# The experts' second product in five fp32r passes of split weights and channels, with the channels' transpose moved ahead of it in each turn

## What is computed

```python
def body(acc, ew):
    w13_e, w2_e, e = ew
    coef = jnp.sum(jnp.where(topk_ids == e, topk_w, 0.0), axis=-1)
    h = _silu_and_mul(x @ w13_e.T)
    acc = acc + (h @ w2_e.T).astype(jnp.float32) * coef[:, None]
    return (acc, None)
...
x = x + 0.5 * _L0_ffn_ref(_layernorm(x, axis=-1), ...)
x = x + _L0_attn_ref(_layernorm(x, axis=-1), ...)
x = x + 0.5 * _L0_ffn_ref(_layernorm(x, axis=-1), ...)
```

## Time and profile before

| | |
|---|---|
| median of 3 runs | 477.45 us (475.16 to 477.74) |
| the profiled execution, its own time | 481.29 us |
| its span, first to last instruction | 479.5 us |
| mean granted TensorE clock | 0.946 of full speed |
| PE busy | 440.3 us, 92% of the span |
| DVE busy | 277.9 us, 58% |
| ACT busy | 168.4 us, 35% |
| slots of f = 0 and of f = 1 | about 73 to 186 us, and 340 to 452 us |

### The profile page before, as it was taken

The page is one execution under the profiler, slowest core; times in us unless marked ns, Lnnn a source line. Parts: engine busy times, 40 slices in busy tenths (PEclk is TensorE's granted clock), DMA queues, the critical chain, the costliest instruction groups (busy, mean ns, idle before and its releaser), DMA issues.

```text
span 479.5 us, 8311 instructions
## 1 busy us (share of the span) xinstructions
PE 440.3 (92%) x2151; PEld 336.8 (70%) x2151; DVE 277.9 (58%) x801; ACT 168.4 (35%) x466; POOL 197.9 (41%) x207
## 2 busy tenths in 40 slices
PE   6889998999999998989979879899899999999890
PEld 4545567998999995534679755455699899999550
DVE  5664665655665562494876444667565566556237
ACT  3221632444444441227556312010244444444210
POOL 0177720444344443630354107785044444444462
PEclk9988998999999998989989768999999999999895
DMA  7999731344344422900000097322334444442192
GB/s 257 385 390 329 244 111 51 118 126 123 123 124 125 121 81 71 411 1 2 0 0 1 2 333 255 117 86 96 90 118 127 121 126 122 125 122 92 56 350 88
DMA packets 40219, 67.35 MB, mean 140 GB/s; under 512 B 5040, under 2 KB 31408, under 8 KB 40176
## 3 DMA queue, kind: packets, MB, share of 16 engines
q1 hardware_dynamic: 32592, 45.05, 29.2%
q0 software_dynamic: 7584, 21.77, 12.9%
HBM read 41.64 MB, written 25.17 MB: 139 GB/s over the span
## 4 chain that ended last, share of the span: by engine, by line
PE 82%; DVE 12%; ACT 2%; issue 2%; DMA 1%; DVEq 0%; ACTq 0%
PE ps L474 17%; PE ps L399 9%; PE ps L422 8%; PE ps L404 7%; PE ps L453 7%; PE ps L449 7%; PE ps L450 6%; PE ps L434 4%; PE ps L461 4%; PE ps L539 3%; DVE X L1101 2%; PE ps L368 2%; PE ps L620 2%; PE ps L355 1%; DVE WR L1100 1%
## 5 line engine op out<-in xcount | busy, mean ns | idle before, releaser
L860 POOL DMA_INDIRECT rows<-ar,idx x94 | 90.3, 960 | 155.5 <-ACT ar L725 152.7
L474 PE MATMUL ps<-W,ar 88*128 x376 | 97.9, 382 | 2.8 <-DVE ar L1078 2.8
L853 POOL DMA_INDIRECT slots<-XR,pos x64 | 67.5, 1055 | 59.3 <-DVE pos L1026 40.4
L1072 DVE SCALAR_TENSOR_TENSOR ar<-ps,XR,ar 128x176 f32<-128x176 f32 x94 | 37.7, 401 | 84.1 <-ACT ar L719 84.1
L449 PE MATMUL ps<-WH,xt 128*128 x188 | 69.3, 369 | 2.8 <-ACT xt L714 1.5
L474 PEld LDWEIGHTS ps<-W,ar 88*128 88x128 f32 x376 | 63.9, 190 | 9.1 <-issue 3.8
L450 PE MATMUL ps<-WL,xt 128*128 x188 | 61.0, 325 | 0.0
L719 ACT ACTIVATE ar<-ps 128x176 f32<-128x176 f32 x94 | 29.9, 318 | 81.8 <-PE ps L453 81.8
L725 ACT ACTIVATE ar<-ps 128x256 f32<-128x256 f32 x94 | 36.2, 385 | 50.8 <-PE ps L474 50.8
L399 PE MATMUL ps<-XT,WS 128*128 128x512 f32 x96 | 52.8, 679 | 1.0 <-ACT sgt L702 1.0
L422 PE MATMUL ps<-WS,ar 128*128 128x256 f32 (+1 forms) x192 | 46.0, 385 | 4.1 <-DVE ar L954 4.1
(11 more groups left out here) (151 smaller groups left out, 596.4 us busy)
## 6 DMA issues: line engine op xcount, KB each, us to landing
XR<-slots SPq DMA_DIRECT2D x94, 144.0 KB, 2.1
WR<-w SPq DMA_DIRECT2D x8, 1408.0 KB, 14.6
WR<-rows SPq DMA_DIRECT2D x16, 512.0 KB, 7.1
W<-w SPq DMA_DIRECT2D x1, 3072.0 KB, 28.7
slots<-zeros SPq DMA_DIRECT2D x1, 2304.0 KB, 12.8
rows<-ar,idx POOLq DMA_INDIRECT x94
X<-x SPq DMA_DIRECT2D x4, 256.0 KB, 4.3
WS<-wsh SPq DMA_DIRECT2D x2, 512.0 KB, 7.8
```

Source lines behind the costliest of these rows:

```text
L474: mm = pe.matmul(ps[:, 2 + i % 2, 0:D], ht[i % 2][:, c * P:(c + 1) * P], w, start=c == 0, stop=c == 1)
L853: pool.indirect_dma_start(out=slots_dram[:, :], out_offset=bass.IndirectOffsetOnAxis(ap=pos[:, t, r:r + 1], axis=0), in_=XR[:, t, :], in_o ...
L860: pool.indirect_dma_start(out=rows_dram[:, :], out_offset=bass.IndirectOffsetOnAxis(ap=idx[:, i:i + 1], axis=0), in_=ys[i % NY], in_offset ...
```

## The change

The second product is made in fp32r with its operands split in two parts each, like the first. The 176 channels are cut into 112 (`FM`) and 64 (`FR`) in place of 88 and 88.

- The weights' first 112 rows become `MH` (fp32r copy, ACT) and `ML` (remainder, DVE). The last 64 rows are loaded twice, one copy below the other, into `RH`, whose lower half DVE turns into the remainder. ACT and DVE do this in `part(u)` at u = 2, 3, 7 and 8 of f = 0. The load of the first 112 rows reuses the memory of the other and so waits for it.
- DVE's product of a slot is two instructions, of 112 columns and of 2 x 64 (the last 64 channels written twice, side by side).
- PE transposes 112 and 128 columns. ACT copies the transposed channels to fp32r (`hh`), and DVE subtracts to get the remainder (`hl`); before, DVE made one copy.
- PE makes five passes of 256 columns in place of two fp32 matmuls. The last two wait for `hl`.
- In each turn `slot_hidden(i-1)` now stands ahead of `slot_out(i-2)`.
- The descriptor memory of GpSimd's transfers is made smaller (`dynamic_dma_scratch_size=2048`), which makes room for the new tiles.

```diff
             for e in range(0, NE, 4):
                 sp.dma_start(WR[:, e:e + 4, :, :], w13[e:e + 4].rearrange("e k p n -> p e k n")).then_inc(s_we[e // 4], 16)
-            sp.dma_start(W2[:, :, :, :], w2.rearrange("e c p n -> p e c n")).then_inc(s_w2, 16)
+            sp.wait_ge(s_rl, len(W2_FIRST))
+            sp.wait_ge(s_rh, len(W2_FIRST))
+            sp.dma_start(MR[0:FM, :, :], w2m).then_inc(s_w2m, 16)
...
             def slot_hidden(f, i):
                 pe.wait_ge(s_hm, TL * f + i + 1)
-                wait(pe, s_htc, TL * f + i - 1)
-                for c in range(2):
-                    mm = pe.transpose(ps[0:KE, 6 + i % 2, c * P:(c + 1) * P], hm[i % 2][:, c * KE:(c + 1) * KE], ident)
-                mm.then_inc(s_ht, 1)
+                wait(pe, s_hl, TL * f + i - 1)
+                pe.transpose(ps[0:FM, 6 + i % 2, 0:P], hm[i % 2][:, 0:FM], ident)
+                pe.transpose(ps[:, 6 + i % 2, P:2 * P], hm[i % 2][:, FM:FM + P], ident).then_inc(s_ht, 1)
...
-                for c in range(2):
-                    w = W2[0:KE, bass.ds(e, 1), c, :].rearrange("p a n -> p (a n)")
-                    mm = pe.matmul(ps[:, 2 + i % 2, 0:D], ht[i % 2][:, c * P:(c + 1) * P], w, start=c == 0, stop=c == 1)
-                mm.then_inc(s_l2, 1)
+                pe.matmul(to, hh[i % 2][main, 0:P], of(MH, main), start=True, stop=False)
+                pe.matmul(to, hh[i % 2][main, 0:P], of(ML, main), start=False, stop=False)
+                pe.matmul(to, hh[i % 2][:, P:2 * P], of(RH, slice(0, P)), start=False, stop=False)
+                pe.wait_ge(s_hl, TL * f + i + 1)
+                pe.matmul(to, hl[i % 2][main, 0:P], of(MH, main), start=False, stop=False)
+                pe.matmul(to, hl[i % 2][rest, P:2 * P], of(RH, rest), start=False, stop=True).then_inc(s_l2, 1)
...
             def part(u):
+                if u in W2_FIRST:
+                    act.wait_ge(s_w2r, 32)
+                    some = slice(*W2_FIRST[u])
+                    act.activation(RH[:, some, :], MR[:, some, :], ACT.Copy).then_inc(s_rh, 1)
+                if u in W2_LAST:
+                    act.wait_ge(s_w2m, 16)
+                    some = slice(*W2_LAST[u])
+                    act.activation(MH[:, some, :], MR[0:FM, some, :], ACT.Copy).then_inc(s_mh, 1)
...
-                    dve.scalar_tensor_tensor(hm[i % 2], ps[:, 4 + i % 2, FE:2 * FE], row[:, bass.ds(e + R_CF, 1)], sg[i % 2],
+                    dve.scalar_tensor_tensor(hm[i % 2][:, 0:FM], ps[:, 4 + i % 2, FE:FE + FM], rate, sg[i % 2][:, 0:FM],
+                                             ALU.mult, ALU.mult)
+
+                    twice = hm[i % 2][:, FM:FM + 2 * FR].rearrange("p (a n) -> p a n", a=2)
+                    dve.scalar_tensor_tensor(twice, spread(ps[:, 4 + i % 2, FE + FM:2 * FE], 1, 2), rate, spread(sg[i % 2][:, FM:FE], 1, 2),
                                              ALU.mult, ALU.mult).then_inc(s_hm, 1)
```

More of the change, by code:

```diff
@@ L101, in aside @@
             return a
-        W2 = sb("W2", [KR, NE, 2, D])
+        RH = sb("RH", [P, NE, D], F32R)
+        MH = sb("MH", [FM, NE, D], F32R)
+        with nc.sbuf_tensor("ML", [FM, NE, D], F32R) as ML:
+            pass
+        MR = sb("MR", [P, NE, D])
         WS1 = sb("WS1", [P, KD, 2 * NJ - 1, P])
@@ L159, in macaron @@
             with nc.sbuf_tensor("xl", [P, 2, D], F32R) as xl_all:
-                pass
+                with nc.sbuf_tensor("hh", [P, 2, D], F32R) as hh_all:
+                    with nc.sbuf_tensor("hl", [P, 2, D], F32R) as hl_all:
+                        pass
         xt = [xt_all[:, h, :] for h in range(2)]
         xl = [xl_all[:, h, :] for h in range(2)]
+        hh = [hh_all[:, h, :] for h in range(2)]
+        hl = [hl_all[:, h, :] for h in range(2)]
         ar = sb("ar", [P, 6 * N])
@@ L171, in macaron @@
         sg = [area(3072 + h * FE, FE) for h in range(2)]
-        hm = [area(3072 + (2 + h) * FE, FE) for h in range(2)]
-        ht = [ar[0:KE, 4480 + h * D:4480 + (h + 1) * D] for h in range(2)]
+        hm = [area(3424 + h * (FM + 2 * FR), FM + 2 * FR) for h in range(2)]
         xs = [XR[:, i, :] for i in range(NX)]
@@ L725, in result, with hidden @@
                     act.activation(ys[i % NY], ps[:, 2 + i % 2, 0:D], ACT.Copy).then_inc(s_y, 1)
+                def hidden(i):
+                    act.wait_ge(s_ht, TL * f + i + 1)
+                    wait(act, s_l2, TL * f + i - 1)
+                    act.activation(hh[i % 2], ps[:, 6 + i % 2, 0:D], ACT.Copy).then_inc(s_hh, 1)
                 turned(0)
@@ L732, in slots @@
                         turned(i + 1)
+                    if 1 <= i <= TL:
+                        hidden(i - 1)
                     if i >= 2:
@@ L959, in part @@
             def part(f, u):
+                if f == 0 and u in W2_FIRST:
+                    dve.wait_ge(s_rh, list(W2_FIRST).index(u) + 1)
+                    some = slice(*W2_FIRST[u])
+                    dve.tensor_tensor(RH[FR:P, some, :], MR[FR:P, some, :], RH[FR:P, some, :].bitcast(F32), ALU.subtract).then_inc(s_rl, 1)
+                if f == 0 and u in W2_LAST:
+                    dve.wait_ge(s_mh, list(W2_LAST).index(u) + 1)
+                    some = slice(*W2_LAST[u])
+                    dve.tensor_tensor(ML[:, some, :], MR[0:FM, some, :], MH[:, some, :].bitcast(F32), ALU.subtract).then_inc(s_ml, 1)
                 for e in range(*PARTED.get(u, (0, 0))):
@@ L1095, in slots @@
                     if 1 <= i <= TL:
-                        turned(i - 1)
+                        rest(i - 1)
             def combine(f, t):
```

44 lines of the change are left out of this document (28 added, 16 removed).

## The result

The changed kernel takes **503.4 us** (median of 4 runs, 498.95 to 504.77), the kernel before 476.5 (4 runs, 475.16 to 477.74). The ratio is 1.055, 95% interval 1.047 to 1.062: slower, where I forecast 471.4 us and gave a slowdown 15 chances in 100. The profiled execution took 504.77 with a span of 503.0; before it was 479.5, so 23.5 us more.

A forecast was written before the change was run, and what follows sets the result against it. PE's own work was taken to set the slot's pace, a DVE cycle close behind. Slots -6.0, then +0.3 +3.3 +1.0 -3.6 -1.0, summed to -6.0 us: 477.45 to 471.4 us, range 463 to 480.

The forecast's parts named there:

- PE's streaming: In a slot, five passes of 256 columns take 0.60 us in place of 0.87; PE alone would need 2.00.
- PE's sequencer: In a slot, it issues the rest only after 453's wait; 453 is ready 2.38 us after the previous wait, before 2.15.
- DVE cycle: In a slot, the chain through silu, DVE's products and remainder to the next 453 grows from 2.01 to 2.14 us.
- slot 2.20: The forecast pace of a slot, 2.20 us in place of 2.27, worth -6.0 us over 2 x 43 slots; chance 0.50.
- rival 1: In the slots, PE's columns alone set the pace: 2.05 to 2.10 us a slot, 462 us in all; chance 0.12.
- DVE's pair: In a slot, DVE's two products put the remainder 0.56 us after the first product starts, against 0.43 before.
- The sum over two slots: In the slots, stretches of 2.38 and 2.03 us follow each other over two slots, giving 2.20 a slot.
- the terms beside the slots: Second pass's first slots +0.3, first pass's start +3.3 and clock +1.0, ends -3.6 and clock -1.0 us.
- rival 3: In the slots, DVE's register load waits for its second product: 2.28 to 2.38 us a slot, about 482; chance 0.13.
- The start: First pass: added ACT and DVE work moves the first 453 from 74.30 to about 77.6, +3.3 us; lower clock +1.0.
- Rival 4: DVE's added work and smaller descriptor memory make GpSimd's dispatch late: two delays hidden, three cost about 2, 474 to 480; chance 0.07.
- The ends: From last 453 to shared unit about 3.6 us in place of 5.45: -3.6 for two passes; better clock -1.0.

The follow-up runs named there:

- a_rows112: The changed kernel with the fifth pass over 112 rows of both operands in place of 64: 474.8 us, ratio to before 0.993.
- b_order: The kernel before with only PE's order changed, the transposes of the hidden channels ahead of the second product: 472.6 us, ratio 0.989.
- b_again: The kernel before, unchanged, run again with a profile: 480.3 us in one run.
- a_pieces: The changed kernel with 112 rows, descriptor memory 4096 and DVE's four long w2 subtractions cut into pieces of two experts: 465.7 us, ratio 0.976.
- b_ring: The kernel before with only the descriptor memory set to 2048 in place of the default: 485.9 us, ratio 1.016.
- a_112_ring4: The changed kernel with 112 rows in the fifth pass and descriptor memory 4096, on another chip: 504.3 us, ratio 0.963.

## Why the prediction was wrong

**PE's streaming (0.60 for five passes).** Wrong for one pass. Four passes go at 0.12, as worked out from the columns. The fifth needs 0.21 + 0.32 where 0.24 was forecast, 0.29 more: times 86, 25 us. In total it measured 28.6 us. That is the first step that failed: "352 columns behave like columns and not like a fixed cost" looked only at columns, and the row count of the stationary went unpriced. The trace of before has such rows, on PE's timeline:

```profile
44.13 1.89 PE L422 MATMUL ps<-WS,ar 128*128 128x256 f32 x8
45.85 1.88 PE L399 MATMUL ps<-XT,WS 128*128 128x512 f32 x4
...
57.98 1.99 PE L422 MATMUL ps<-WS,ar 64*128 64x256 f32 x8
59.90 1.55 PE L399 MATMUL ps<-XT,WS 128*128 128x512 f32 x3
```

Eight passes of 256 columns take 45.85 - 44.13 = 1.72 us with 128 rows and 59.90 - 57.98 = 1.92 with 64. The granted clock is 1.00 in both stretches. The 0.20 more per group of eight (a change there, and one back) would have given 17 us over 86 slots, and the sign of the whole forecast. I hadn't looked at this line.

**PE's sequencer and the DVE cycle (slot 2.20).** Also wrong, on the other side. With the fault of the fifth pass gone the slot is 2.07 to 2.08: the pace of rival 1 (2.05 to 2.10, which I gave 0.12). The chain that ended last in `a_rows112` shows a slot whose 468 had to wait, and the next 468:

```profile
117.33 0.59 PE ps L468 x2
...
119.60 0.38 PE ps L468 x2
```

They are 2.27 apart where I had 2.38, and in that chain the pieces between them are all PE's own: the sequencer's path of 2.38 isn't there. DVE's pair costs 0.51 where I had 0.56. The sum over two slots, (2.38 + 2.03)/2, took two paths from one slot that had waited for the steady state. It underrated the gain by 86 x 0.12 = 10 us. That PE's columns alone set the 2.07 isn't shown either: in the slot of `a_rows112` shown above the DVE cycle takes as long (0.58 to the silu, 0.46 to the product, 0.51 to the remainder, 0.41 for it, 0.11 to the next 468), and the two passes of 468 take 0.38 where they took 0.33 in the changed kernel.

**Three slips in the working**, which changed little. 1.5 + 0.1 + 0.11 + 4 x 0.16 is 2.35 and not 2.38, which gives 2.19 a slot. (113.5 - 113.2)/2 is 0.15 and not 0.12. And the terms beside the slots cancel (0.3 + 3.3 + 1.0 - 3.6 - 1.0 = 0.0), so by this sum any slot above 2.27 makes the kernel slower, not only one from 2.31 on, as rival 3 has it.

**The start (+3.3, clock +1.0).** The work of ACT and DVE was right: `ML` ended at 73.83 (forecast 73.9), the last `WL` at 75.44 (75.6), the clock cost 1.0. But these didn't set the start. The dispatch did: +12.8 in place of +3.3. That is the second step that failed: the wait that ends last there is the one for the dispatch, which the sum put at nothing.

**Rival 4 (dispatch).** The mechanism was right in both halves, and the size and the chance were not. I had "two such delays hidden, three cost about 2": there were 9.7 us of longer dispatches (42.27 against 32.61 busy) and 6.7 of waiting for the descriptor memory, 16.7 us later in all, against 3.7 of slack (before, 11.6 us lay between the last dispatch's end and the first silu, and 7.9 are enough after). I priced the descriptor memory at nothing, since no row of before showed a wait for it; how many of 32 dispatches in a row fit in it wasn't asked. The Trainium skill, "SBUF — State Buffer", section "Who interferes with whom", puts the conflict down to a DVE operation with two SBUF inputs against a GpSimd operation that reads SBUF, but infers that such a `tensor_tensor` leaves descriptor writing alone. By these runs the indirect dispatch, which reads its row numbers from SBUF, is held by just such operations, and by several in a row. The trace of before had it too: the dispatch of 3.71 us was held by three `WL` subtractions. The timeline of GpSimd and DVE there:

```profile
319.87 3.71 POOL L853 DMA_INDIRECT slots<-XR,pos  x1 [0.30 <-issue]
320.27 2.48 DVE L966 TENSOR_TENSOR WL<-WR,WH 128x704 fp32r<-128x704 f32 x3
```

It ended at 323.58, and the run at 322.75, 0.83 earlier. Read so, the row says that a run can hold a dispatch for its whole length, and the change adds runs of up to 5 us.

**The ends (-3.6, clock -1.0).** Right: -3.6, and `b_order` shows that the order alone gives it. The clock there rose from 0.72 to 1.00, as said. What it gave back shows in the four matmuls at the start of the first unit behind each end: 2.93 and 3.24 us before (185.96 to 188.89, 451.56 to 454.80), 1.82 and 1.82 after (203.15 to 204.97, 475.33 to 477.15), so 2.5 in place of 1.0. But in `b_again`, the same kernel before, the first of them took 1.72 (183.51 to 185.23), so it was there in only some executions. And behind the second end the program's end didn't gain it: from the unit's start to the last instruction it took 27.9 us before and 27.6 after.

With 112 rows, memory of 4096 and the shorter subtractions together (`a_pieces`), the change gives 465.7 us, 12 less than the kernel before in the same comparison (478.0).

## What to carry to other kernels

Price a pass by its rows as well as its columns: here one with 64 rows between passes of 112 and 128 lost its weight prefetch on both sides (0.3 us), and over 96 or 112 rows it cost nothing extra, where the added rows hold what does no harm. Before work is added to DVE, look for GpSimd dispatches that run at that time, and keep two-input SBUF operations short or behind them. A setting that frees memory is a part of the change like any other: count how many dispatches fit in it, when the last of them lands, and who waits for the end of the dispatch.

## What the runs showed of the hardware that I had not expected

- A pass of 64 rows costs a slot 0.31 us more than one of 96 or 112: 0.09 in front of it (0.21 against 0.12), 0.20 behind it (0.32 against 0.12), and some in the pass that follows, less a little that is won back at 468.
- Descriptor memory of 2048 held 14 dispatches of 128 rows, 4096 held 28. The next one waited 2.2 to 6.7 us, until 0.67 (with 2048) or 0.84 us (with 4096) after the last of them had landed, though the first had landed long before (27.0 against 44.5 in `b_ring`).
- A dispatch held by DVE ended 0.83 to 0.84 us after the end of a subtraction with both inputs in SBUF: mostly of one, but in the longest cases (3.4 to 5.2 us) of the last of an unbroken run.
- On one chip engines stood still for 11 to 28 us during the dispatch, ScalarE for 18 and DVE for 12 of them with their inputs there in `a_112_ring4`, with the kernel before at 524.8 us in place of 477.
